# Self-attention on one core: GpSimd takes the rounding and the remainder of the first tile of probabilities

## The chip, the cores and the metric

One core of one Trainium2 chip. The metric is the device time of one execution of the kernel in microseconds (us).

## The reference

The input x is 8 sequences of 512 tokens with 256 channels, in float32. Two transformer layers follow each other. The first is a cross-attention layer (16 heads of 16, context of 64 tokens with 192 channels) and an MLP. The second starts with the self-attention that this change is about:

```python
def _attn(xq, xc, Wq, Wk, Wv, Wo, bo):      # HEADS 16, D_HEAD 64, xq = xc = layer norm of x
    q = (xq @ Wq).reshape(B, N, HEADS, D_HEAD)
    k = (xc @ Wk).reshape(B, S, HEADS, D_HEAD)
    v = (xc @ Wv).reshape(B, S, HEADS, D_HEAD)
    scores = jnp.einsum("bnhd,bshd->bhns", q, k) * D_HEAD ** -0.5
    attn = jax.nn.softmax(scores, axis=-1)
    out = jnp.einsum("bhns,bshd->bnhd", attn, v).reshape(B, N, HEADS * D_HEAD)
    return out @ Wo + bo
x = _attn(_ln(x, g1, b1), _ln(x, g1, b1), Wq1, Wk1, Wv1, Wo1, bo1) + x
```

A second cross-attention (on the context) and a gated MLP follow.

## The kernel before, in words

Every engine has a queue of its own, written out by hand, and waits for the others at counted events (`event`, `wait_ge`). To keep float32 accuracy with products in the faster float32r type, every operand is split in two: a rounded half, made by a copy (`act_copy` on ScalarE, `pool_copy` on GpSimd, line 159), and a remainder, the difference between the value and its rounded half (`dve_rest`, line 162, on VectorE; `pool_rest`, line 165, on GpSimd). A product is then three matmuls (`mm3`, lines 146 to 148): high by high, high by rest, rest by high.

The self-attention runs over 64 steps (`loop3`): 8 sequences by 8 pairs of heads. In step `s` three things overlap, each on another pair of heads: the pair `t = s` has its scores and exponentials computed, the next pair `u = s + 1` is projected (queries, keys, values) and its largest scores are found, and the pair before, `d = s - 1`, is multiplied with its values. Each step has four parts, `j = 0` to `3`, one per tile of 128 keys. A tile of probabilities is 128 keys by 1024 (two heads by 512 queries), and goes this way:

1. TensorE makes the scores in two parts (`scores`, lines 1348 and 1352); the second part waits for the negated maxima of the pair.
2. ScalarE takes the exponential (line 1500) into one of two buffers, `pst3[n % 2]`. It may start once the remainder of the tile two before has been made, since that read the same buffer.
3. The tile is rounded into `P3[0]`: by ScalarE for `j` = 1 and 2, by GpSimd for `j` = 0 and 3. The product with the values of the pair before must have read the old tile (`d3_mm`).
4. VectorE makes the remainder of all four tiles into `P3[1]` (`rests`, line 1582, by the helper of line 162). Its queue takes the remainder of tile 3 early in the next step.
5. TensorE multiplies both with the values, one step later (`values`).

VectorE's queue in a step is: remainders of the next queries (line 1569, two of 64x512, one input in PSUM), the reciprocals of the sums (line 1615), the remainder of the previous step's tile 3, remainders of the next keys (line 1573, two), remainder of the next values (two of 128x256), remainder of tile 0, in even steps an addition to x (line 1636), the largest scores of the next pair (line 1588, a reduction of 128x1024 from PSUM), and so on with the remainders of tiles 1 and 2 between the reductions; in odd steps the addition to x stands near the end. TensorE's `largest` (line 1386) makes the scores that these reductions read and waits for the remainders of the next queries and keys. After the fourth reduction TensorE transposes the maxima (line 152) and ScalarE negates them.

GpSimd's queue in a step is: two copies of the next keys (64x512 each, `k3_dup`), the rounding of tile 0, then at `j = 2` the product of the previous output with the reciprocals (line 1697, waits for a DMA), its rounding and its remainder (128x512), and the rounding of tile 3. Every eighth step (`p == 6`, an even step) also normalises the next sequence: an addition to x that GpSimd starts at the end of the step before (line 283), and a rounding and a remainder of 128x1024.

SP's queue issues the DMAs of the sums and reciprocals, which wait for events of VectorE and ScalarE.

Of the kernel before, what the change touches and what calls it, by code (L numbers as in the profile page):

```python
# [102 lines left out]
def f32(ap):  # L103
    return ap.bitcast(FP)
# [6 lines left out]
def build(nc, x, ctx_in, par, con, bias, wts, out):  # L111
    es = ExitStack()
    with es:  # L113
# [291 lines left out]
        with nc.sbuf_tensor("R3", [128, 24576], FR) as r, nc.sbuf_tensor("F3", [128, NALL - 24576], FP) as g:  # L405
# [4 lines left out]
            P3 = ra.pair(4, 2 * NT)  # L410
# [789 lines left out]
        p3_act, p3_pool, p3_lo = event("p_act", 2 * N3), event("p_pool", 2 * N3), event("p_lo", 4 * N3)  # L1200
# [53 lines left out]
        def pool_values(b, half):  # L1254
            pool.wait_ge(vw_hi, 2 * b - 4 + half)
            v = vw_b[b % 2][:, 4 * half:4 * half + 4]
            pool_rest(v[:, :, 1], f32(v)[:, :, 1], v[:, :, 0]).then_inc(vw_lo.sem, 1)

# [75 lines left out]
        def pe_attention1():  # L1334
# [54 lines left out]
            def values(d, j):  # L1389
                pe.wait_ge(p3_lo, 4 * d + j)  # L1390
                pe.wait_ge(v3_lo, 2 * (d // 2) + j // 2)
                if j == 0:
                    pe.wait_ge(d3_out, d - 1)
                    pe.wait_ge(gelu, NM - 1)
                vh, vl = v3_s[(d // 2) % 2]
                for h in range(2):
                    cs = slice(64 * h, 64 * h + 128)
                    m = mm3(bank(4 + h), (vh[:, j, d % 2, cs], vl[:, j, d % 2, cs]),
                            [v[:, j, NT * h:NT * h + NT] for v in P3], j == 0, j == 3)
                m.then_inc(d3_mm.sem, 1)  # L1400
# [77 lines left out]
        def act_attention1():  # L1478
# [17 lines left out]
            def exponent(t, j):  # L1496
                n = 4 * t + j
                act.wait_ge(c3_mm, n)
                act.wait_ge(p3_lo, n - 2)
# [62 lines left out]
        def dve_attention1():  # L1562
# [13 lines left out]
            def rests(n):  # L1576
                if 0 <= n < 4 * N3:
                    if n % 4 in (1, 2):
                        dve.wait_ge(p3_act, 2 * (n // 4) + n % 4 - 1)
                    else:  # L1580
                        dve.wait_ge(p3_pool, 2 * (n // 4) + n % 4 // 3)
                    dve_rest(P3[1][:, n % 4, :], pst3[n % 2], P3[0][:, n % 4, :]).then_inc(p3_lo.sem, 1)
# [72 lines left out]
        def pool_attention1():  # L1655
# [22 lines left out]
            for s in loop3:  # L1678
# [9 lines left out]
                for j in range(4):  # L1688
                    if ok(u, N3) and j == 0:
# [13 lines left out]
                    if ok(t, N3) and j in (0, 3):  # L1703
                        pool.wait_ge(e3, 4 * t + j)
                        pool.wait_ge(d3_mm, 4 * (t - 1) + j)
                        pool_copy(P3[0][:, j, :], pst3[j % 2]).then_inc(p3_pool.sem, 1)
# [57 lines left out]
        def sp_attention2():  # L1764
# [3 lines left out]
            for i in loop4:  # L1768
                b = i // 4
                if i == 2:  # L1770
                    sp.wait_ge(p3_lo, 4 * N3 - 1)
# [365 lines left out]
```

## Time and profile before

| | |
|---|---|
| median of 3 runs | 2293.42 us (2293.42 to 2293.97) |
| the profiled execution | 2292.69 us, span 2290.9 us |
| mean granted TensorE clock | 0.98 |
| TensorE busy | 2121.8 us (93%) |
| VectorE busy | 1608.8 us (70%) |
| ScalarE busy | 1482.3 us (65%) |
| GpSimd busy | 1070.5 us (47%) |

The span runs from the first to the last instruction of the profiled execution; the time also has what lies around it. The shares are means over stages with different limits: products, first layer, the self-attention loop, and the second half of the second layer. The times of rows count from the start of the span. A row of a stretch gives from and to, its length, the busy time (and instructions) of PE, PEld, DVE, ACT and POOL, the granted clock, the DMA share and GB/s. A row of the waits gives who waited for whom, the total in us, how often, and the longest. A row of a timeline gives the start, the duration, the engine, the line (often a helper's), the shapes, how many equal instructions were merged into it, and in brackets the engine's idle time before it and what ended that. PE is TensorE (PEld its weight loads), DVE is VectorE, ACT is ScalarE, POOL is GpSimd. A TensorE row lasts longer than the distance to the next one, because matmuls are pipelined.

### The profile page before, as it was taken

What the parts mean: (1) busy time and instruction counts of PE and PEld (TensorE: products, weight loads), DVE (VectorE), ACT (ScalarE), POOL (GpSimd) and SP (SyncE); (2) the same over time, 40 slices, a digit from 0 to 9 for tenths busy, and PEclk for the clock granted to TensorE, in tenths of its full rate; (3) what the DMA queues carried; (4) which work ended last, traced back from release to release, by engine and by line L of the source; (5) the groups of instructions that cost most, each with busy time, mean ns of one, the idle gap of its engine ahead of it and who ended that gap; (6) DMA issues with size and microseconds to landing.
All of it is one profiled execution on the core that took longest, in us unless ns stands there. A gap on an engine that the chain in (4) does not pass through costs nothing. (4 is left out here: it accounts for less than half of the span.)

```text
span 2290.9 us, 31305 instructions
## 1 busy us (share of the span) xinstructions
PE 2121.8 (93%) x11628; PEld 1771.6 (77%) x11628; DVE 1608.8 (70%) x2345; ACT 1482.3 (65%) x2154; POOL 1070.5 (47%) x819
## 2 busy tenths in 40 slices
PE   6868999988899999999999999999997799999998
PEld 4657888876687778777777777777776689888987
DVE  5576767753787787777877778778776766666553
ACT  5546888754777777777777777777774355554431
POOL 2154544441354454454544545545454665656432
PEclk8989999998999999999999999999999999999999
DMA  6810000010000100001001000010004411111000
GB/s 212 297 43 5 22 22 22 20 66 33 19 24 16 37 15 24 24 15 34 15 15 34 15 29 24 15 33 15 24 26 165 138 44 53 56 56 47 10 10 19
DMA packets 84280, 102.67 MB, mean 45 GB/s; under 512 B 29664, under 2 KB 61152, under 8 KB 83616
## 3 DMA queue, kind: packets, MB, share of 16 engines
q1 hardware_dynamic: 84128, 100.66, 13.3%
q8 instruction: 93, 1.52, 0.3%
q14 instruction: 59, 0.48, 0.1%
HBM read 65.50 MB, written 33.82 MB: 43 GB/s over the span
## 5 line engine op out<-in xcount | busy, mean ns | idle before, releaser
L146 PE MATMUL PS<-R 128*128 128x512 f32 (+1 forms) x2944 | 1026.4, 349 | 77.1 <-DVE R L162 46.1
L148 PE MATMUL PS<-R 128*128 128x512 f32 (+1 forms) x2944 | 996.5, 338 | 0.0
L147 PE MATMUL PS<-R 128*128 128x512 f32 (+1 forms) x2944 | 995.8, 338 | 0.0
L146 PEld LDWEIGHTS PS<-R 128*128 128x128 f32 x2944 | 565.8, 192 | 189.9 <-DVE R L162 55.3
L156 ACT ACTIVATE R<-PS 64x512 fp32r<-64x512 f32 (+4 forms) x860 | 460.1, 548 | 239.7 <-PE PS L1805 129.4
L148 PEld LDWEIGHTS PS<-R 128*128 128x128 f32 x2944 | 565.1, 192 | 60.4
L147 PEld LDWEIGHTS PS<-R 128*128 128x128 f32 x2944 | 566.9, 193 | 54.4
L162 DVE TENSOR_TENSOR R<-F,R 128x1024 fp32r<-128x1024 f32 (+2 forms) x416 | 465.2, 1123 | 44.2 <-ACT R L156 22.4
L159 POOL TENSOR_SCALAR R<-F 128x1024 fp32r<-128x1024 f32 (+1 forms) x295 | 266.2, 904 | 284.0 <-DVE F L1958 149.3
L1500 ACT ACTIVATE F<-PS 128x1024 f32<-128x1024 f32 x256 | 263.1, 1028 | 170.3 <-DVE R L162 115.1
L159 POOL TENSOR_SCALAR R<-R 64x512 fp32r<-64x512 f32 x128 | 142.8, 1129 | 391.4 <-ACT R L156 391.4
L1588 DVE TENSOR_REDUCE F<-PS 128x2 f32<-128x1024 f32 x256 | 301.4, 1214 | 14.1 <-PE PS L1386 14.1
L162 DVE TENSOR_TENSOR R<-PS,R 128x512 fp32r<-128x512 f32 (+3 forms) x348 | 181.0, 542 | 160.9 <-ACT R L156 160.3
L165 POOL TENSOR_TENSOR R<-F,R 128x512 fp32r<-128x512 f32 (+2 forms) x126 | 229.6, 1824 | 31.0 <-ACT R L156 22.4
L1569 DVE TENSOR_TENSOR R<-PS,R 64x512 fp32r<-64x512 f32 x128 | 88.0, 688 | 220.1 <-ACT R L156 220.1
L156 ACT ACTIVATE R<-F 128x1024 fp32r<-128x1024 f32 (+2 forms) x246 | 200.5, 829 | 61.2 <-PE PS L148 56.0
L156 ACT ACTIVATE F<-PS 64x512 f32<-64x512 f32 (+3 forms) x280 | 160.2, 593 | 50.4 <-PE PS L148 40.5
L1386 PE MATMUL PS<-R 128*128 128x512 f32 x512 | 164.0, 402 | 7.2 <-ACT F L156 4.9
L1352 PE MATMUL PS<-R 128*128 128x512 f32 x512 | 162.7, 399 | 7.8 <-ACT R L156 6.5
L1348 PE MATMUL PS<-R 128*128 128x512 f32 x512 | 165.9, 405 | 2.6 <-ACT F L1500 2.6
L1134 POOL TENSOR_TENSOR F<-F 128x1024 f32<-128x1024 f32 x32 | 67.9, 2123 | 165.4 <-DVE F L1048 165.4
L1697 POOL TENSOR_TENSOR F<-F 128x512 f32<-128x512 f32 x64 | 82.7, 1292 | 119.6 <-DMA F<-sd 119.6
(89 smaller groups left out, 1990.9 us busy)
## 6 DMA issues: line engine op xcount, KB each, us to landing
F<-sd SPq DMA_DIRECT2D x128, 128.0 KB, 2.8
xs<-F SPq DMA_DIRECT2D x16, 512.0 KB, 2.6
F<-xs SPq DMA_DIRECT2D x16, 512.0 KB, 3.6
gd<-F SPq DMA_DIRECT2D x8, 768.0 KB, 3.6
vd<-F SPq DMA_DIRECT2D x8, 768.0 KB, 5.9
R<-gd SPq DMA_DIRECT2D x6, 1024.0 KB, 5.5
R<-vd SPq DMA_DIRECT2D x6, 1024.0 KB, 5.7
F<-in_x SPq DMA_DIRECT2D x8, 512.0 KB, 5.7
```

Of the source, the lines that this page charges most:

```text
L146: nc.tensor.matmul(o, L[0], Rr[0], start=start, stop=False, skip_group_check=share)
L147: nc.tensor.matmul(o, L[0], Rr[1], start=False, stop=False, skip_group_check=share)
L148: return nc.tensor.matmul(o, L[1], Rr[0], start=False, stop=stop, skip_group_check=share)
L156: return nc.scalar.activation(o, i, ACT.Identity, **k)
L159: return nc.gpsimd.tensor_scalar(o, i, 1.0, 1.0, ALU.mult, ALU.mult)
L162: return nc.vector.tensor_tensor(o, i, f32(hi), ALU.subtract)
L165: return nc.gpsimd.tensor_tensor(o, i, f32(hi), ALU.subtract)
L1348: nc.tensor.matmul(bank(h), ka[i][h][:, kk], qa[i][h], start=True, stop=False)
L1352: m = nc.tensor.matmul(bank(h), kb[i][h][:, kk], qb[i][h], start=False, stop=True)
L1386: m = nc.tensor.matmul(bank(b0 + h), qa[i][h][:, 128 * q:128 * q + 128], ka[i][h], start=True, stop=True)
L1500: nc.scalar.activation(pst3[n % 2], bank(0, 2), ACT.Exp, scale=0.125).then_inc(e3.sem, 1)
L1588: nc.vector.tensor_reduce(M3[:, q, 0:128:64], bank(b0, 2).rearrange("p (a b) -> p a b", a=2), AX.X, ALU.max).then_inc(b3_max.sem, 1)
```

## The change

For tile 0 alone, GpSimd now makes both the rounded half and the remainder. It does so at the start of its part `j = 0`, ahead of the two copies of the next keys; before, it rounded the tile behind these copies, and VectorE made the remainder. VectorE makes the remainders of tiles 1 to 3. Since two engines now finish remainders, the event `p3_lo` is split in two, and `wait_rest3` picks the right one for a tile. The exponential that reuses a buffer, the value products and SP's first weight loads of the next stage wait by it.

```diff
--- before.py
+++ after.py
@@ -1197,7 +1197,8 @@
         nm3_mm, nm3_neg = event("nm_mm", N3), event("nm_neg", N3)
         c3_mm, e3 = event("c_mm", 4 * N3), event("exp", 4 * N3)
 
-        p3_act, p3_pool, p3_lo = event("p_act", 2 * N3), event("p_pool", 2 * N3), event("p_lo", 4 * N3)
+        p3_act, p3_pool = event("p_act", 2 * N3), event("p_pool", 2 * N3)
+        p3_lo_pool, p3_lo_dve = event("p_lo_pool", N3), event("p_lo_dve", 3 * N3)
         d3_mm, d3_sum, d3_out = event("d_mm", 4 * N3), event("d_sum", N3), event("d_out", N3)
         rec3, mul3, o3_hi, o3_lo = event("rec", N3), event("o_mul", N3), event("o_hi", N3), event("o_lo", N3)
         o3_mm, o3_add = event("o_mm", N3), event("x_add", N3)
@@ -1255,6 +1256,12 @@
             pool.wait_ge(vw_hi, 2 * b - 4 + half)
             v = vw_b[b % 2][:, 4 * half:4 * half + 4]
             pool_rest(v[:, :, 1], f32(v)[:, :, 1], v[:, :, 0]).then_inc(vw_lo.sem, 1)
+
+        def wait_rest3(queue, n):
+            if n % 4 == 0:
+                queue.wait_ge(p3_lo_pool, n // 4)
+            else:
+                queue.wait_ge(p3_lo_dve, 3 * (n // 4) + n % 4 - 1)
 
         def tail3(s, j):
 
@@ -1387,7 +1394,7 @@
                 m.then_inc(b3_mm.sem, 1)
 
             def values(d, j):
-                pe.wait_ge(p3_lo, 4 * d + j)
+                wait_rest3(pe, 4 * d + j)
                 pe.wait_ge(v3_lo, 2 * (d // 2) + j // 2)
                 if j == 0:
                     pe.wait_ge(d3_out, d - 1)
@@ -1496,7 +1503,7 @@
             def exponent(t, j):
                 n = 4 * t + j
                 act.wait_ge(c3_mm, n)
-                act.wait_ge(p3_lo, n - 2)
+                wait_rest3(act, n - 2)
                 nc.scalar.activation(pst3[n % 2], bank(0, 2), ACT.Exp, scale=0.125).then_inc(e3.sem, 1)
 
             def value(u):
@@ -1574,12 +1581,12 @@
                                                 ).then_inc(k3_lo.sem, 1)
 
             def rests(n):
-                if 0 <= n < 4 * N3:
-                    if n % 4 in (1, 2):
+                if 0 <= n < 4 * N3 and n % 4 > 0:
+                    if n % 4 < 3:
                         dve.wait_ge(p3_act, 2 * (n // 4) + n % 4 - 1)
                     else:
-                        dve.wait_ge(p3_pool, 2 * (n // 4) + n % 4 // 3)
-                    dve_rest(P3[1][:, n % 4, :], pst3[n % 2], P3[0][:, n % 4, :]).then_inc(p3_lo.sem, 1)
+                        dve.wait_ge(p3_pool, 2 * (n // 4) + 1)
+                    dve_rest(P3[1][:, n % 4, :], pst3[n % 2], P3[0][:, n % 4, :]).then_inc(p3_lo_dve.sem, 1)
 
             def largest(u, q, b0):
                 dve.wait_ge(b3_mm, 4 * u + q)
@@ -1686,6 +1693,12 @@
                     for b_ in (6, 7):
                         pool.wait_ge(x_out[x_at(0, b_)], store_no[0, b_])
                 for j in range(4):
+                    if ok(t, N3) and j == 0:
+                        pool.wait_ge(e3, 4 * t)
+                        pool.wait_ge(d3_mm, 4 * (t - 1))
+                        pool_copy(P3[0][:, 0, :], pst3[0]).then_inc(p3_pool.sem, 1)
+                        pool.wait_ge(p3_pool, 2 * t)
+                        pool_rest(P3[1][:, 0, :], pst3[0], P3[0][:, 0, :]).then_inc(p3_lo_pool.sem, 1)
                     if ok(u, N3) and j == 0:
                         for h in range(2):
                             pool.wait_ge(k3_hi, 2 * u + h)
@@ -1700,10 +1713,10 @@
                         pool_copy(o3_s[f % 2][0], OA).then_inc(o3_hi.sem, 1)
                         pool.wait_ge(o3_hi, f)
                         pool_rest(o3_s[f % 2][1], OA, o3_s[f % 2][0]).then_inc(o3_lo.sem, 1)
-                    if ok(t, N3) and j in (0, 3):
-                        pool.wait_ge(e3, 4 * t + j)
-                        pool.wait_ge(d3_mm, 4 * (t - 1) + j)
-                        pool_copy(P3[0][:, j, :], pst3[j % 2]).then_inc(p3_pool.sem, 1)
+                    if ok(t, N3) and j == 3:
+                        pool.wait_ge(e3, 4 * t + 3)
+                        pool.wait_ge(d3_mm, 4 * (t - 1) + 3)
+                        pool_copy(P3[0][:, 3, :], pst3[1]).then_inc(p3_pool.sem, 1)
                     for job in weights3_at(s, j):
                         pool_weight(job)
                     for _ in range(early4_pool.get(tail3(s, j), 0)):
@@ -1768,7 +1781,8 @@
             for i in loop4:
                 b = i // 4
                 if i == 2:
-                    sp.wait_ge(p3_lo, 4 * N3 - 1)
+                    wait_rest3(sp, 4 * N3 - 4)
+                    wait_rest3(sp, 4 * N3 - 1)
                     for k in range(4):
                         sp_weight(g5, k)
                     sp_load(3, 2, xs)
```

## Rows read from the trace of the kernel before

**Rows 1.** Busy time by stretch: an odd step, an even step, the whole loop.
```profile
1181.99:1199.82 17.83, 17.81 (x91) 14.45 (x90) 13.33 (x16) 13.79 (x20) 8.42 (x7) 1.00 0.06 16
1199.82:1218.36 18.54, 17.47 (x88) 14.04 (x87) 14.12 (x16) 13.70 (x21) 7.55 (x7) 1.00 0.12 44
573.00:1756.00 1183.00, 1130.17 (x5625) 910.97 (x5626) 908.74 (x1119) 884.56 (x1291) 567.74 (x475) 1.00 0.08 26
```
**Rows 2.** The waits of the loop (573 to 1756 us), the longest.
```profile
POOL R L159 <- ACT R L156: 370.1, 63, 12.5
```
**Rows 3.** TensorE in order of time: start us, us, what, xcount [idle <-releaser].
```profile
1187.76 0.70 PE L1386 MATMUL PS<-R 128*128 128x512 f32 x2
...
1194.06 0.39 PE L148 MATMUL PS<-R 128*128 128x512 f32 x1
1194.46 0.36 PE L146 MATMUL PS<-R 128*128 128x256 f32 x1
...
1207.70 0.63 PE L1352 MATMUL PS<-R 128*128 128x512 f32 x2
1208.34 0.70 PE L1386 MATMUL PS<-R 128*128 128x512 f32 x2
...
1213.20 0.39 PE L148 MATMUL PS<-R 128*128 128x512 f32 x1
1214.52 0.65 PE L152 MATMUL PS<-F 128*128 128x128 f32 x4 [0.93 <-DVE F L1588]
...
1217.16 0.73 PE L1352 MATMUL PS<-R 128*128 128x512 f32 x2
```
**Rows 4.** VectorE in order of time, the same two steps.
```profile
1185.00 1.17 DVE L162 TENSOR_TENSOR R<-F,R 128x1024 fp32r<-128x1024 f32 x1
1186.20 1.41 DVE L1573 TENSOR_TENSOR R<-PS,R 64x512 fp32r<-64x512 f32 x2
...
1189.68 2.35 DVE L1588 TENSOR_REDUCE F<-PS 128x2 f32<-128x1024 f32 x2
...
1202.83 1.17 DVE L162 TENSOR_TENSOR R<-F,R 128x1024 fp32r<-128x1024 f32 x1
...
1205.70 0.76 DVE L162 TENSOR_TENSOR R<-PS,R 128x256 fp32r<-128x256 f32 x2 [0.26 <-ACT R L156]
1206.38 1.21 DVE L162 TENSOR_TENSOR R<-F,R 128x1024 fp32r<-128x1024 f32 x1
1207.51 0.68 DVE L1636 TENSOR_TENSOR F<-PS,F 128x512 f32<-128x512 f32 x1
```
**Rows 5.** ScalarE in order of time, the even step.
```profile
1204.10 1.03 ACT L1500 ACTIVATE F<-PS 128x1024 f32<-128x1024 f32 x1 [0.78 <-DVE R L162]
...
1212.57 1.03 ACT L1500 ACTIVATE F<-PS 128x1024 f32<-128x1024 f32 x1 [0.99 <-DVE R L162]
1213.63 2.27 ACT L156 ACTIVATE F<-PS 1x512 f32<-1x512 f32 x4
```
**Rows 6.** GpSimd in order of time, the even step.
```profile
1207.74 1.29 POOL L1697 TENSOR_TENSOR F<-F 128x512 f32<-128x512 f32 x1 [1.66 <-DMA F<-sd]
1209.12 0.62 POOL L159 TENSOR_SCALAR R<-F 128x512 fp32r<-128x512 f32 x1
1209.82 1.29 POOL L165 TENSOR_TENSOR R<-F,R 128x512 fp32r<-128x512 f32 x1
1213.75 1.04 POOL L159 TENSOR_SCALAR R<-F 128x1024 fp32r<-128x1024 f32 x1 [2.64 <-ACT F L1500]
```
**Rows 7.** A norm step (1272.8 to 1293.1 us): GpSimd, then VectorE, by time.
```profile
1272.33 2.40 POOL L283 TENSOR_TENSOR F<-F 128x1024 f32<-128x1024 f32 x1 [3.71 <-DVE F L262]
...
1287.49 2.37 POOL L165 TENSOR_TENSOR R<-F,R 128x1024 fp32r<-128x1024 f32 x1
...
1272.80 0.68 DVE L1569 TENSOR_TENSOR R<-PS,R 64x512 fp32r<-64x512 f32 x1 [0.55 <-ACT R L156]
...
1288.16 2.79 DVE L162 TENSOR_TENSOR R<-F,R 128x1024 fp32r<-128x1024 f32 x1
```

## Prediction

> **What bounds the kernel now.** I read the stretches first, then the waits, then two neighbouring steps engine by engine. The stretch from 573 to 1756 us is the self-attention loop: 1183 of the span's 2290.9 us for 64 steps, 18.5 us each with its edges [rows 1]. TensorE is busy in 1130 of the 1183 us; no other engine passes 909. In one odd step (17.83 us from 1181.99) and the even one behind it (18.54 us from 1199.82) TensorE is busy for all but 0.02 and 1.07 us. So the loop is TensorE's instruction stream plus the few places where its next instruction is not yet released. VectorE's 909 us don't bound by themselves; what matters is which of its results TensorE waits for.
>
> The waits [rows 2] say where GpSimd has room: it idles 370 us, 5.9 us each time, ahead of its copies, for ScalarE. Most of that lies ahead of the keys' copies, where the change puts its new work.
>
> TensorE's queue [rows 3] has a few soft places in two steps. Odd: the first L1386 (the products that the maxima are taken from) starts at 1187.76, in rhythm. The output product starts at 1194.46, while the 0.23 us rhythm from 1194.06 would have it at 1194.29: with the broken rhythm behind it 0.24 us, for GpSimd's rounded output. Even: an L1386 starts at 1208.34, 0.18 us later than the pair at 1207.70 needs, because VectorE's addition to x (L1636) ends only at 1208.19 [rows 4]; and the transposes start at 1214.52, 1.09 us later than the rhythm from 1213.20, for VectorE's last maximum. The last of these is worth little: ScalarE begins four copies of 2.27 us together at 1213.63 [rows 5], as soon as the value products of 1213.20 are done, and two more follow that L1352 waits for, at 1217.16. These 3.96 us from value product to L1352 hold whatever VectorE does.
>
> **The change, part by part.** Tiles 1 to 3 stay as they are. The waits that change their semaphore cost nothing: what they wait for comes earlier than before. For tile 0:
>
> VectorE loses its remainder, 1.21 us at 1206.38 in the even step [rows 4], the same in the odd one. If nothing else moved, the x addition would come early enough to give back 0.18 us and 0.07 of broken rhythm, and ScalarE's chain leaves the transposes 0.05: 0.3 us an even step. The output wait of the odd step could give its 0.24. That is the whole prize: (0.3 + 0.24) x 32 = 17 us.
>
> GpSimd rounds tile 0 ahead of the keys' copies. Behind exponential 3, which ends at 1212.57 + 1.03 = 1213.60 [rows 5], its rounding starts at 1213.75 [rows 6], 0.15 later. So behind exponential 0 (1199.82 + 1.03 = 1200.85) it starts at 1201.00 and ends 1.04 later. The value product that must have read the old tile lies at the start of the step and is over. 0.08 us on (as from 1209.12 + 0.62 to 1209.82) the new remainder starts, at about 1202.13. It takes what the same instruction on the same shape takes in the layer norm, 2.37 us [rows 7], to 1204.50.
>
> **The collision.** VectorE wants its remainder of the previous tile 3 at 1202.83, in the odd step at 1185.00 [rows 4]: both 3.0 us after exponential 0 starts. GpSimd's will have started 0.70 us before. Rows of the norm step show this very pair [rows 7]: GpSimd's started at 1287.49 for 2.37 us, VectorE's at 1288.16, and VectorE's took 2.79 us instead of 1.17; it ended 1.09 us after GpSimd's. The first to start runs, the other stands. The Trainium skill, SBUF — State Buffer, "Who interferes with whom", has this as a rule, and it speaks against the change: a VectorE instruction with two SBUF inputs and a GpSimd one that reads SBUF want one port pair, and the first holds it for its whole length. By that rule VectorE would end a full instruction behind GpSimd, 0.1 us later than the row, and the sum would be some 3 us higher; the trace agrees but for that 0.1. VectorE's other operations around there have one input in PSUM; one of them (1272.80, 0.68 us) lies inside a GpSimd addition of 2.40 us [rows 7] and keeps its length. Only the remainder collides.
>
> It ends, then, at 1204.50 + 1.09 = 1205.59 instead of 1202.83 + 1.17 = 1204.00: **1.59 us late**. Behind it in VectorE's queue stand the keys' remainders (L1573), the values' rests, the x addition and the maxima; and ScalarE's exponential 1, which started at 1204.10 after 0.78 us of waiting for that same remainder [rows 5].
>
> Odd step. L1573 starts at 1186.20 + 1.59 and takes 1.41, to 1189.20. L1386 needs it and wanted 1187.76; with 0.07 for the release it starts at 1189.27: TensorE stands 1.51 us. Then VectorE has caught up, because tile 0's remainder is gone: the first maximum, at 1189.68 before, now waits for TensorE. The output product comes 1.5 us later, so its 0.24 vanish. Net +1.27.
>
> Even step. Exponential 1 starts at 1205.69; the values' copies and rests follow it as before, the rests at 1205.70 + 1.59 for 0.76, to 1208.05; the x addition then runs to about 1208.65 instead of 1208.19. L1386 starts at 1208.80 instead of 1208.34: +0.46. Behind that the maxima keep pace, and the fixed 3.96 us carry the 0.46 into the next step.
>
> The keys' copies (2.3 us together without a block, 1.1 more with VectorE first behind GpSimd's remainder) end near 1207.9. Their readers are the scores of the next step: nothing. The product with the reciprocals (L1697) waited for its DMA until 1207.74: 0.1 to 0.2 late, hidden by the same step's TensorE delay. SP's queue is not passed: the reciprocal that starts its DMAs stands ahead of the blocked remainder.
>
> Every eighth step is the norm step, even. There GpSimd starts with the addition at 1272.33 for 2.40 us [rows 7], which moves tile 0's rounding to about 1274.8 and the remainder to 1275.9. VectorE's wants 3.0 us after 1272.80, at 1275.8: a tie, VectorE first by 0.1. Then nothing is late and the 0.25 at the x addition is gained, some -0.2 us. If GpSimd wins, about +1.
>
> **Sum.** Eight steps: 4 x 1.27 + 3 x 0.46 - 0.2 = 6.3 us; times eight, 50 us. The profiled execution took 2292.69 us (span 2290.9 and 1.8 around it), 0.7 below the median of 2293.42; 2292.7 + 50 = **2343 us**, 2.2% more.
>
> **Rivals.** (A) No collision, because VectorE's remainder is first: the prize of 17 us, 2276 us. For it: 0.7 us of lead is not much beside what moves elsewhere. Against it: both engines count from the same exponential, and GpSimd would have to start 0.7 us later behind it than the 0.15 of [rows 5, 6]. 6%. (B) The collision is there, and TensorE's slack of 1.1 us in two steps takes it up: within 0.2% of 2293. For it the even step's 1.09; against it that this wait lies behind the delay, and that the odd step has no slack ahead of L1386. 3%. (C) Exponentials and maxima re-form around the stall and it counts by half: 2318 us. 15%. (D) Neither delay is caught up: with exponential 1 late, tile 1's remainder runs into GpSimd's output remainder (1.29 us at 1209.82 [rows 6]) in every step, and the tie in the norm step is lost. Then odd steps cost 1.5, even ones 1.0, the norm step 1: 4 x 1.5 + 3 x 1.0 + 1 = 10 us in eight steps, 80 in all, 2373 us. 12%. (E) The sum above: 64%.
>
> **How the numbers follow.** Within 0.2% (4.6 us) a measurement of this kernel can't be told from no change. Faster is A, 6%; no change is B, 3%; slower is the rest, 91%. The unknown inputs of E are the tie (-0.2 or +1 a norm step, 10 us) and the even step (0.3 to 0.9 for 0.46, 15 us). The range takes these and C in, and leaves out A, B and the far part of D: 2316 to 2362 us.
>
> **What the changed profile should show.** GpSimd's 128x1024 remainders in the loop: 64 more, near 2.4 us. VectorE's: 192 instead of 256, a third of them (those behind the reciprocal) near 2.6 us instead of 1.17. In the odd step L1386 directly behind L1573, with 1.5 us of TensorE idle ahead that names VectorE. Odd steps of 19.1 us, even ones of 19.0. If VectorE's remainders stay near 1.2 us, the collision was wrong and A holds. If they are long and the odd step still takes 17.8, it is B. If the even step has grown by 1 or more, D.

## The result, and the profile after

The changed kernel takes 2337.34 us in the median of four runs, the kernel before 2293.42 us. One of the four was in a slow state (2652.71 us, at a mean granted clock of 0.745 where the others have 0.98); the other three took 2334.98 to 2339.24 us. Those three, against the runs of the kernel before, give a ratio of 1.0192 with a 95% interval of 1.0172 to 1.0212: 1.9% slower. The profiled execution took 2339.24 us, with a span of 2337.4 us.

The stretches, in the columns of [rows 1]: an odd step, the even one behind it, the whole loop.

```profile
1205.66:1224.79 19.13, 17.86 (x92) 14.60 (x91) 14.59 (x15) 13.65 (x20) 9.83 (x8) 1.00 0.06 15
1224.79:1243.72 18.93, 17.74 (x88) 14.11 (x87) 14.53 (x15) 13.64 (x20) 9.83 (x8) 1.00 0.12 43
573.00:1802.00 1229.00, 1136.07 (x5626) 915.29 (x5625) 943.22 (x1056) 880.54 (x1291) 689.83 (x539) 1.00 0.08 25
```

The two steps took 17.83 and 18.54 us and now take 19.13 and 18.93. In the odd step nearly all of the growth is idle time of TensorE, 1.27 us where it was 0.02. In the even step the idle time went from 1.07 to 1.19 us, and the other 0.27 us show as busy time (17.74 for 17.47). The 256 exponentials give the loop as a whole (count, duration, first and last start), before and after:

```profile
L1500 ACT ACTIVATE F<-PS x256: 1007/1027/1035, 573.4 to 1741.8; 128x1024 f32<-128x1024 f32 x128
L1507 ACT ACTIVATE F<-PS x256: 1004/1027/1033, 575.1 to 1788.0; 128x1024 f32<-128x1024 f32 x128
```

From first to last start that is 1212.9 us, where it was 1741.8 - 573.4 = 1168.4: 44.5 us, nearly all of the 46.6 us by which the two profiled executions differ. From each exponential 0 to the next (steps are numbered from 0), the 31 odd steps have a median of 19.08 us (17.82 before) and give 37.7 us, the 24 even ones 18.94 (18.55) and 8.3 us, the eight norm steps 20.10 (20.33) and -1.9 us. Exponential 0 starts these two steps at 1205.66 and 1224.79. In order of time, VectorE (L1580 was L1573 in the kernel before, L1595 was L1588, L1643 was L1636):

```profile
1208.68 2.71 DVE L162 TENSOR_TENSOR R<-F,R 128x1024 fp32r<-128x1024 f32 x1
1211.41 1.41 DVE L1580 TENSOR_TENSOR R<-PS,R 64x512 fp32r<-64x512 f32 x2
...
1213.76 2.57 DVE L1595 TENSOR_REDUCE F<-PS 128x2 f32<-128x1024 f32 x2
1216.24 1.98 DVE L162 TENSOR_TENSOR R<-F,R 128x1024 fp32r<-128x1024 f32 x1
...
1227.80 2.71 DVE L162 TENSOR_TENSOR R<-F,R 128x1024 fp32r<-128x1024 f32 x1
...
1232.88 0.68 DVE L1643 TENSOR_TENSOR F<-PS,F 128x512 f32<-128x512 f32 x1
```

GpSimd:

```profile
1206.77 1.05 POOL L159 TENSOR_SCALAR R<-F 128x1024 fp32r<-128x1024 f32 x1 [4.65 <-ACT F L1507]
1207.91 2.39 POOL L165 TENSOR_TENSOR R<-F,R 128x1024 fp32r<-128x1024 f32 x1
...
1225.90 1.04 POOL L159 TENSOR_SCALAR R<-F 128x1024 fp32r<-128x1024 f32 x1 [5.09 <-ACT F L1507]
1227.03 2.40 POOL L165 TENSOR_TENSOR R<-F,R 128x1024 fp32r<-128x1024 f32 x1
1229.40 2.18 POOL L159 TENSOR_SCALAR R<-R 64x512 fp32r<-64x512 f32 x2
```

GpSimd's remainder starts at 1207.91, VectorE's wants to at 1208.68, and takes 2.71 us instead of 1.17 [rows 4]. It ends at 1211.39, 1.09 us after GpSimd's 1210.30. The even step is the same: 1227.03 against 1227.80. The keys' remainders (L1580) start 1.54 us later than they otherwise would. TensorE, where L1393 is the former L1386 [rows 3]:

```profile
1212.97 0.70 PE L1393 MATMUL PS<-R 128*128 128x512 f32 x2 [1.27 <-DVE R L1580]
...
1233.71 0.70 PE L1393 MATMUL PS<-R 128*128 128x512 f32 x2
...
1239.52 0.66 PE L152 MATMUL PS<-F 128*128 128x128 f32 x4 [0.56 <-DVE F L1595]
```

In the odd step L1393 stands until 1212.97, 7.31 us after exponential 0 where it was 5.77 (1187.76 - 1181.99), and the row names the keys' remainder. In the even step the second L1393 starts 8.92 us after exponential 0, 8.52 before (1208.34 - 1199.82). ScalarE's exponential 1 in the even step waits 2.32 us, 0.78 before [rows 5]:

```profile
1230.61 1.03 ACT L1507 ACTIVATE F<-PS 128x1024 f32<-128x1024 f32 x1 [2.32 <-DVE R L162]
```

The waits of the loop. GpSimd's long wait ahead of the keys' copies [rows 2] is gone, since its own work stands there and now waits for the exponential, and a wait is new that the loop before does not have at all:

```profile
POOL R L159 <- ACT F L1507: 260.1, 56, 10.6
...
PE PS L1393 <- DVE R L1580: 42.5, 45, 1.6
```

In the norm step, the pair started in the other order by 0.04 us, VectorE (first row) ahead of GpSimd:

```profile
1304.02 1.17 DVE L162 TENSOR_TENSOR R<-F,R 128x1024 fp32r<-128x1024 f32 x1
...
1304.06 3.41 POOL L165 TENSOR_TENSOR R<-F,R 128x1024 fp32r<-128x1024 f32 x1
```

There VectorE keeps its 1.17 us and GpSimd pays, 3.41 instead of 2.4 us.

Such meetings are not new. The two engines meet in nearly every step of the kernel before as well. In its even step VectorE's remainder of tile 1 starts while GpSimd makes the remainder of the output (1209.82 to 1211.11 [rows 6]):

```profile
1210.37 1.82 DVE L162 TENSOR_TENSOR R<-F,R 128x1024 fp32r<-128x1024 f32 x1
```

It takes 1.82 us instead of 1.21 and ends 1.08 us after GpSimd's. Of the 22 even steps from 4 to 60 that are not norm steps, VectorE is held at tile 1 in 21. That is part of why the transposes wait 0.9 to 1.3 us there for its last maximum; in the one step without it (60) they wait 0.32 us. In the odd step VectorE is first (1191.95 for 1.22 us), and GpSimd's remainder of the output, 0.22 us behind, takes 2.14 us instead of 1.29. In the changed kernel VectorE comes later, so in the odd step it is now VectorE that is held (1216.24, 1.98 us).

### The profile page after: what moved, and what is told of

The parts are those of the page before. It is cut to its first block and busy times, and to the rows that moved or that the text cites. A ratio compares the mean times of both kernels' runs of the same rounds, so it can differ in the third digit from the quotient of the medians.

```text
span 2337.4 us, 31306 instructions
## 1 busy us (share of the span) xinstructions
PE 2130.4 (91%) x11628; PEld 1778.1 (76%) x11628; DVE 1642.0 (70%) x2281; ACT 1477.8 (63%) x2154; POOL 1192.3 (51%) x883
## 5 line engine op out<-in xcount | busy, mean ns | idle before, releaser
L146 PEld LDWEIGHTS PS<-R 128*128 128x128 f32 x2944 | 566.0, 192 | 178.6 <-DVE R L162 54.6
L148 PEld LDWEIGHTS PS<-R 128*128 128x128 f32 x2944 | 565.6, 192 | 61.3
L147 PEld LDWEIGHTS PS<-R 128*128 128x128 f32 x2944 | 567.2, 193 | 55.0
L162 DVE TENSOR_TENSOR R<-F,R 128x1024 fp32r<-128x1024 f32 (+1 forms) x352 | 489.6, 1397 | 45.6 <-ACT R L156 26.0
L165 POOL TENSOR_TENSOR R<-F,R 128x1024 fp32r<-128x1024 f32 (+2 forms) x190 | 366.0, 1928 | 39.6 <-ACT R L156 25.7
L1595 DVE TENSOR_REDUCE F<-PS 128x2 f32<-128x1024 f32 x256 | 305.1, 1216 | 20.0 <-PE PS L1393 16.1
L1393 PE MATMUL PS<-R 128*128 128x512 f32 x512 | 165.9, 405 | 48.9 <-DVE R L1580 42.5
L1393 PEld LDWEIGHTS PS<-R 128*128 128x128 f32 x512 | 88.7, 188 | 91.0 <-issue 68.5
L159 POOL TENSOR_SCALAR R<-R 64x512 fp32r<-64x512 f32 x128 | 128.3, 1017 | 20.9 <-ACT R L156 20.9
```

The lines of the kernel that those rows point to most:

```text
L146: nc.tensor.matmul(o, L[0], Rr[0], start=start, stop=False, skip_group_check=share)
L147: nc.tensor.matmul(o, L[0], Rr[1], start=False, stop=False, skip_group_check=share)
L148: return nc.tensor.matmul(o, L[1], Rr[0], start=False, stop=stop, skip_group_check=share)
L159: return nc.gpsimd.tensor_scalar(o, i, 1.0, 1.0, ALU.mult, ALU.mult)
L162: return nc.vector.tensor_tensor(o, i, f32(hi), ALU.subtract)
L165: return nc.gpsimd.tensor_tensor(o, i, f32(hi), ALU.subtract)
```

## The experiments

The kernel before ran beside every set on the same chip; a ratio is to those runs, with its 95% interval. "Before" is the kernel before the change, "the change" the changed one.

**1. The remainder behind the keys' copies** (on the change). The same work on GpSimd, at another place of its queue.

```diff
-                        pool.wait_ge(p3_pool, 2 * t)
-                        pool_rest(P3[1][:, 0, :], pst3[0], P3[0][:, 0, :]).then_inc(p3_lo_pool.sem, 1)
                     if ok(u, N3) and j == 0:
                         for h in range(2):
...
+                    if ok(t, N3) and j == 0:
+                        pool.wait_ge(p3_pool, 2 * t)
+                        pool_rest(P3[1][:, 0, :], pst3[0], P3[0][:, 0, :]).then_inc(p3_lo_pool.sem, 1)
```

> The changed kernel with one thing moved: GpSimd rounds tile 0 ahead of the keys' copies as in the change, but makes its remainder behind them. Collision theory: GpSimd's remainder now runs about 5.3 to 7.7 us after exponential 0, where VectorE has only instructions with one input in PSUM, so VectorE's 192 remainders go back to about 1.2 us except where they meet the output's remainder, L1580 and L1393 are back in rhythm, and what is left is the 17 us of prize that the prediction worked out: 2276 us, between 2268 and 2288. Rival (the remainder on GpSimd costs by itself, through later releases of the exponential of tile 2 or through GpSimd's fuller queue ahead of L1710): 2310 us or more, as the work that GpSimd does is the same as in the change.

Measured: 2288.42 us, ratio 0.9979 (0.9969 to 0.9989). The whole loss is gone and a little gained, with all of tile 0 still on GpSimd; the rival falls at its price of 2310. But 5 us are not the 17 of the prize. In the odd step VectorE now reaches its remainder of tile 1 sooner, and meets GpSimd's output chain there (L1711 is the former L1697); the last row is TensorE's in another odd step:

```profile
1189.56 1.58 DVE L162 TENSOR_TENSOR R<-F,R 128x1024 fp32r<-128x1024 f32 x1
...
1188.76 1.29 POOL L1711 TENSOR_TENSOR F<-F 128x512 f32<-128x512 f32 x1 [0.62 <-DMA F<-sd]
1190.14 1.48 POOL L159 TENSOR_SCALAR R<-F 128x512 fp32r<-128x512 f32 x1
...
677.95 0.36 PE L146 MATMUL PS<-R 128*128 128x256 f32 x1 [0.53 <-POOL R L165]
```

VectorE's remainder (1189.56) waits for the end of the product (1190.05), and then GpSimd's rounding takes 1.48 us instead of 0.62. So the output's remainder, for which TensorE waits in the odd step, mostly ends about 12.3 us after exponential 0, as before: the odd step gains nothing (17.87 us in the median for 17.82). In eight odd steps it is worse. There GpSimd's queue also has a small operation for the next sequence's norm (L256), behind the new remainder; the output's remainder ends at 12.8, TensorE stands 0.53 us for it, as in the last row, and the step takes 18.3 us. That is some 4 us in all, and is the rival's mechanism at a small price: GpSimd's fuller queue. The even steps gained what the prediction said, 0.28 us (18.27 for 18.55 in the median), where VectorE was not held at tile 1.

**2. One wait against the meeting** (on the change).

```diff
                         pool.wait_ge(p3_pool, 2 * t)
+                        pool.wait_ge(p3_lo_dve, 3 * t - 1)
```

> The changed kernel with one wait added: GpSimd's remainder of tile 0 starts only when VectorE has made the remainder of the previous tile 3. Collision theory: VectorE's remainder takes 1.17 us and L1393 of the odd step has its rhythm back (no 1.4 us of idle), but GpSimd's remainder runs at 4.2 to 6.6 us after exponential 0, the keys' copies at 6.7 to 8.9, and the product with the reciprocals is about 0.9 us later than its DMA would let it; the odd step's output product waits up to that. So 2276 plus up to 28: 2300 us, between 2280 and 2312. Rival (GpSimd's work itself is what delays, not the meeting of the two): no lower than the changed kernel, 2337 us or more, as everything on GpSimd is later still.

Measured: 2290.59 us, ratio 0.9989 (0.9979 to 0.9999). GpSimd's remainder and the keys' copies are both later than in the change, and the loss is gone; the rival falls. The number lies nearer to before than my 2300, for a reason in GpSimd's rows:

```profile
1182.69 1.17 DVE L162 TENSOR_TENSOR R<-F,R 128x1024 fp32r<-128x1024 f32 x1
...
1184.01 2.41 POOL L165 TENSOR_TENSOR R<-F,R 128x1024 fp32r<-128x1024 f32 x1 [2.16 <-DVE R L162]
1186.38 1.21 POOL L159 TENSOR_SCALAR R<-R 64x512 fp32r<-64x512 f32 x2
```

VectorE's remainder takes 1.17 us, GpSimd's follows, and then both keys' copies together take 1.21 us, where they took 2.29 before. Alone they cost 0.6 us each. The 2.29 already held a meeting with the same remainder of VectorE, in which GpSimd's copy was the one that stood, although the profile has it start 0.05 us ahead (in the even step, 1202.78 against 1202.83).

**3. The rounding alone** (on before): `pool_copy` of tile 0 ahead of the keys' copies, its remainder on VectorE as before.

```diff
+                    if ok(t, N3) and j == 0:
+                        pool.wait_ge(e3, 4 * t)
+                        pool.wait_ge(d3_mm, 4 * (t - 1))
+                        pool_copy(P3[0][:, 0, :], pst3[0]).then_inc(p3_pool.sem, 1)
                     if ok(u, N3) and j == 0:
...
-                    if ok(t, N3) and j in (0, 3):
+                    if ok(t, N3) and j == 3:
```

> The kernel before with only the first half of the change: GpSimd rounds tile 0 ahead of the keys' copies, VectorE makes all four remainders as before. The rounding ends at about 2.2 us after exponential 0, before VectorE's remainder of tile 3 wants to start at 3.0. Collision theory: nothing collides and nothing on a path moves, 2293 us within 4. Rival (moving the rounding ahead is part of the cost, by the keys' copies or by the wait for the value product): slower by 5 to 20 us.

Measured: 2292.62 us, ratio 1.0001 (0.9989 to 1.0013). That half of the change costs nothing that can be told from noise.

**4. The same place, but only writing** (on before, with the edit of 3 and, behind the rounding, this).

```diff
+                        for k in range(3):
+                            pool.wait_ge(p3_try, 3 * t + k - 1)
+                            nc.gpsimd.memset(f32(P3[1])[:, 0, 0:(1024, 1024, 512)[k]], 0.0).then_inc(p3_try.sem, 1)
```

VectorE's `rests` waits for the third before it makes tile 0's remainder over it.

> The kernel before with the rounding of tile 0 ahead of the keys' copies and, behind it, three fills of constants (1024, 1024 and 512 columns, about 2.4 us together) into the tile that VectorE's remainder overwrites later; VectorE makes all four remainders. GpSimd is as busy in the same place as in the change, and the keys' copies as late, but it reads nothing there. If it is GpSimd's reading of SBUF that VectorE's remainder meets: VectorE's remainders stay at 1.17 us and the time at 2293 within 5. Rival 1 (any GpSimd instruction in that place blocks, writing too): VectorE's remainders behind the reciprocal grow to 2.2 us or more and the time goes above 2340, since VectorE still has all four tiles. Rival 2 (the late keys' copies cost): above 2300 with VectorE's remainders at 1.17.

Measured: 2291.47 us, ratio 0.9995 (0.9985 to 1.0006). VectorE, then GpSimd:

```profile
1183.97 1.17 DVE L162 TENSOR_TENSOR R<-F,R 128x1024 fp32r<-128x1024 f32 x1
...
1183.06 2.55 POOL L1698 MEMSET R<- 128x1024 f32 x3
1185.58 1.20 POOL L159 TENSOR_SCALAR R<-R 64x512 fp32r<-64x512 f32 x2
```

GpSimd is busy from 1183.06 to 1185.61, VectorE's remainder lies inside that time and takes 1.17 us. Writing alone does not block it, and keys' copies that start at 1185.58 cost nothing. The Trainium skill, SBUF — State Buffer, "Who interferes with whom", says that an instruction of VectorE with two inputs in SBUF does not contend with one of GpSimd that only writes. These rows agree. A fill is not a remainder without its reading, so that it is the reading that blocks rests on this pair of operations.

**5. The collision without the relief** (on before, with the edit of 3): GpSimd makes the remainder early, as in the change, and VectorE makes it again in its old place.

```diff
+                        pool.wait_ge(p3_pool, 2 * t)
+                        pool_rest(P3[1][:, 0, :], pst3[0], P3[0][:, 0, :]).then_inc(p3_try.sem, 1)
...
+                    if n % 4 == 0:
+                        dve.wait_ge(p3_try, n // 4)
```

> The kernel before, with the rounding of tile 0 ahead of the keys' copies and GpSimd's remainder of tile 0 behind it, as in the change; but VectorE makes all four remainders as before, that of tile 0 a second time in its old place. This is the collision without the relief. Collision theory: VectorE's remainder behind the reciprocal takes 2.7 us, and as tile 0's remainder is still queued behind it, the 1.59 us are not caught up in either step: 1.5 us in 32 odd and 24 even steps, 84 us, 2377 us, between 2360 and 2395. Rival (the cost comes from readers that now wait for GpSimd's remainder, not from the meeting): as these readers wait for VectorE again here, no more than 2300.

Measured: 2432.74 us, ratio 1.0609 (1.0593 to 1.0625). The rival falls, but 142 us are much more than my 84, and outside my bounds. The late queue runs into a second meeting. VectorE, then GpSimd, in an odd step:

```profile
1213.47 2.73 DVE L162 TENSOR_TENSOR R<-F,R 128x1024 fp32r<-128x1024 f32 x1
...
1218.57 2.25 DVE L162 TENSOR_TENSOR R<-F,R 128x1024 fp32r<-128x1024 f32 x1
...
1212.70 2.41 POOL L165 TENSOR_TENSOR R<-F,R 128x1024 fp32r<-128x1024 f32 x1
...
1218.44 1.29 POOL L1706 TENSOR_TENSOR F<-F 128x512 f32<-128x512 f32 x1 [1.19 <-DMA F<-sd]
```

The first is the known one (2.73 us). The second remainder (tile 0's, 1218.57) now lands on GpSimd's product with the reciprocals (1218.44 to 1219.73) and takes 2.25 us. A delay of 1.6 us became 2.6, and the odd steps take 20.3 us for 17.8. The even steps from 4 to 60 come in three lengths, where the kernel before has one near 18.55: 20.1 us (5 of 22), in which tile 0's remainder is not held, 21.1 (11) and 22.7 (6), in which it is. What parts the last two was not followed up.

**6. Half the remainder** (on before, with the edit of 3): GpSimd makes the first 512 columns early, VectorE the other 512 late. Every reader of the tile waits for both.

```diff
+                        pool_rest(P3[1][:, 0, 0:512], pst3[0][:, 0:512], P3[0][:, 0, 0:512]).then_inc(p3_half.sem, 1)
...
+                    c0 = 0 if n % 4 else 512
+                    dve_rest(P3[1][:, n % 4, c0:], pst3[n % 2][:, c0:], P3[0][:, n % 4, c0:]).then_inc(p3_lo.sem, 1)
```

> The kernel before, with the rounding of tile 0 ahead of the keys' copies and behind it GpSimd's remainder of only the first 512 columns of tile 0 (1.29 us instead of 2.4); VectorE makes the other 512 columns in its old place. If VectorE is held exactly as long as GpSimd's instruction still runs: its remainder ends at 2.30 + 1.29 + 1.09 = 4.68 us after exponential 0 instead of 4.18, 0.5 us late instead of 1.6 (a duration of about 1.7 us), the odd step grows by 0.3 to 0.5 and the even one by nothing: 2302 us, between 2295 and 2310. Rival (each meeting has a fixed toll, whatever its length): VectorE's remainder 2.4 us or more and 2315 to 2340 us.

Measured: 2294.21 us, ratio 1.0011 (1.0002 to 1.002). VectorE, then GpSimd:

```profile
1204.31 1.61 DVE L162 TENSOR_TENSOR R<-F,R 128x1024 fp32r<-128x1024 f32 x1
...
1203.54 1.29 POOL L165 TENSOR_TENSOR R<-F,R 128x512 fp32r<-128x512 f32 x1
1204.81 2.17 POOL L159 TENSOR_SCALAR R<-R 64x512 fp32r<-64x512 f32 x2
```

GpSimd's ends at 1204.83, VectorE's 1.09 us later; 1.61 us, near the 1.7 expected. So the toll is the rest of the other's instruction (0.52 us, for 0.44 of delay; in the change 1.62, for 1.54) and not a fixed one. The time lies just below my bounds: of a delay of 0.45 us, 0.15 are left in an odd step (17.97 us for 17.82) and nothing in an even one.

**7 and 8. ScalarE's order** (7 on experiment 1, 8 on before): in even steps the negated maxima before the output's copies.

```diff
                         act_copy(OB[0:1, :], bank(5)[0:1, :]).then_inc(d3_sum.sem, 1)
+                        if ok(u, N3) and s % 2 == 0:
+                            act.wait_ge(nm3_mm, u)
...
+                            for h in range(2):
+                                m = act_copy(qb[u % 2][h][64:65, :], bank(odd_bank(u))[64 * h:64 * h + 1, :], scale=-1.0)
+                            m.then_inc(nm3_neg.sem, 1)
                         act.wait_ge(o3_lo, d - 1)
...
-                    if ok(u, N3) and j == 3:
+                    if ok(u, N3) and j == 3 and not (ok(d, N3) and s % 2 == 0):
```

> e1_rest_behind_keys (remainder of tile 0 on GpSimd behind the keys' copies) with ScalarE reordered in the even steps: the two negated maxima come before the two copies of the output (OA) instead of after them. It tests the step of the prediction that says that ScalarE's fixed chain, not VectorE's last maximum, sets L1359 in even steps. If so, L1359 comes 1.0 us earlier, the value products behind it then wait about 0.6 us for the output copies, and an even step loses 0.4 us: 2277 us, between 2268 and 2285. Rival (the value products' wait takes back all of it, or the chain was not the bound): 2288 within 3.

> The kernel before with ScalarE's reordering alone. There the transposes wait 1.1 us for VectorE's last maximum, so that the negated maxima can come only 0.8 us earlier than before, and the value products 0.2 us earlier: 2287 us, between 2280 and 2293. If the reordering gains as much here as on top of the remainder's move (10 us or more), the two are independent and VectorE's maxima were not the next bound behind ScalarE.

Measured: 2298.56 us (1.0034, 1.0022 to 1.0046) and 2304.01 us (1.0059, 1.0045 to 1.0072). Both miss, to the slow side. ScalarE in an even step of 7 (1200.80 to 1219.89):

```profile
1214.64 1.19 ACT L156 ACTIVATE F<-PS 1x512 f32<-1x512 f32 x2
1216.23 1.19 ACT L156 ACTIVATE R<-PS 1x512 fp32r<-1x512 f32 x2 [0.41 <-PE PS L152]
1217.45 1.20 ACT L156 ACTIVATE F<-PS 64x512 f32<-64x512 f32 x2
1218.67 1.19 ACT L156 ACTIVATE R<-PS 64x512 fp32r<-64x512 f32 x2
1219.89 1.03 ACT L1507 ACTIVATE F<-PS 128x1024 f32<-128x1024 f32 x1
```

The negated maxima (1216.23) now wait 0.41 us for the transposes with two output copies and two of the next queries still behind them, and exponential 0 stands behind all of these. Before, the output's copies filled that wait. An order that helps one reader put idle time into the engine that was itself without a break. But 7 has two kinds of even steps. In 11 of the 22 from 4 to 60 GpSimd's remainder of the output starts first and VectorE's remainder of tile 1 is held (2.15 to 2.34 us); the transposes are late, as in these rows, and the step takes 19.0 to 19.2 us. In ten VectorE is first, ScalarE doesn't wait for the transposes, and TensorE stands 0.4 to 0.6 us for the output's copies instead; the step takes 18.4 to 18.5, still more than the 18.26 of experiment 1. In 8, as before, VectorE is held in all but one, and nearly all take 19.0 to 19.3.

**9 and 10. The output's copies on VectorE** (9 on experiment 1, 10 on before), in even steps.

```diff
-                        act.wait_ge(o3_lo, d - 1)
...
+                        if s % 2:
+                            act.wait_ge(o3_lo, d - 1)
...
+                    if ok(d, N3) and j == 3 and s % 2 == 0:
+                        dve.wait_ge(d3_mm, 4 * d + 3)
+                        dve.wait_ge(o3_lo, d - 1)
+                        nc.vector.tensor_copy(OA[0:64, :], bank(4)[0:64, :])
+                        nc.vector.tensor_copy(OA[64:128, :], bank(5)[64:128, :]).then_inc(d3_out.sem, 1)
```

> e1_rest_behind_keys, and in even steps the two copies of the output (OA, 64x512 each) go from ScalarE to VectorE, behind its remainder of tile 2, into the time that the change freed there. e1's profile shows ScalarE without a break from 1212.06 to the next exponential 0 (1216.78) and TensorE waiting 1.0 us for it ahead of L1359, while VectorE idles 3.5 us. e7 showed that changing ScalarE's order only moves the wait; this takes 1.2 us off it. If ScalarE's chain is what bounds the even step of e1: L1359 about 1.0 and exponential 0 about 0.8 us earlier, 24 to 32 times: 2264 us, between 2258 and 2275. Rival (another wait takes over at once, as in e7, or VectorE's copies delay what stands behind them): 2283 or more.

> The kernel before with the output's copies of even steps on VectorE, as in e9. Here VectorE still makes tile 0's remainder, and its last maximum holds the transposes until 1214.5, behind which the next projection and exponential 0 stand. So the relief of ScalarE can give only 0.1 to 0.3 us an even step: 2287 us, between 2281 and 2293. That this and e1 alone give little but e9 gives 25 us or more would show that the two chains of the even step, VectorE's and ScalarE's, are nearly as long as each other, and that the prize of the change is cut by the second. Rival (ScalarE's chain alone bounds): 2270 or less here.

Measured: 2286.97 us (0.9982, 0.9972 to 0.9992) and 2294.15 us (1.0007, 0.9998 to 1.0015). Both miss: experiment 9 gave little where I expected 24 us, 10 gave nothing. But the profile of 9 has two kinds of even steps, ten of 17.4 to 17.5 us and twelve of 18.4 to 18.6 among the 22 from 4 to 60. For each: VectorE's remainder of tile 1, GpSimd's remainder of the output, TensorE's transposes.

```profile
1203.66 2.27 DVE L162 TENSOR_TENSOR R<-F,R 128x1024 fp32r<-128x1024 f32 x1
...
1203.56 1.29 POOL L165 TENSOR_TENSOR R<-F,R 128x512 fp32r<-128x512 f32 x1
...
1208.25 0.66 PE L152 MATMUL PS<-F 128*128 128x128 f32 x4 [1.23 <-DVE F L1596]
...
1384.66 1.22 DVE L162 TENSOR_TENSOR R<-F,R 128x1024 fp32r<-128x1024 f32 x1
...
1384.84 2.19 POOL L165 TENSOR_TENSOR R<-F,R 128x512 fp32r<-128x512 f32 x1
...
1388.20 0.66 PE L152 MATMUL PS<-F 128*128 128x128 f32 x4 [0.18 <-DVE F L1596]
```

In the first GpSimd started 0.10 us ahead, VectorE's took 2.27 us, and the transposes stood 1.23 us. In the second VectorE started 0.18 us ahead, GpSimd paid (2.19), and the transposes waited 0.18 us. Eleven of the twelve long steps are like the first (GpSimd 0.03 to 0.3 us ahead, VectorE's remainder 2.1 to 2.3 us; in the twelfth GpSimd's product with the reciprocals, late, holds it), and all ten short ones like the second.

The profile of 10 says why it gained nothing. It is the kernel before in this respect: in 19 of the 22 steps VectorE's remainder of tile 1 is held (1.7 to 2.1 us), and they take 18.3 to 18.7 us. In the other three VectorE is first, and they take 17.85 to 17.92 us. One of those, VectorE, then GpSimd:

```profile
768.94 1.21 DVE L162 TENSOR_TENSOR R<-F,R 128x1024 fp32r<-128x1024 f32 x1
...
769.01 2.30 POOL L165 TENSOR_TENSOR R<-F,R 128x512 fp32r<-128x512 f32 x1
```

**11 and 12. The second meeting ordered too** (11 on experiment 9, 12 on experiment 1).

```diff
                         pool.wait_ge(o3_hi, f)
+                        if ok(t, N3) and s % 2 == 0:
+                            wait_rest3(pool, 4 * s + 1)
```

> e9_output_on_vector with one wait added: in even steps GpSimd's remainder of the output starts only when VectorE has made its remainder of tile 1. In e9's profile the two want to start within 0.1 us of each other in each even step, and whichever is first there makes a step of about 17.4 or of 18.4 us: where GpSimd is first, VectorE's remainder takes 2.27 us and its last maximum, and with it the transposes, come 1.05 us later; where VectorE is first nothing waits for GpSimd's. If the order of starting is the cause, the wait makes all even steps short: some half of 24 steps by 1.0 us and the spread gone, 10 to 15 us below e9: 2273 us, between 2264 and 2280. Rival (the two kinds of steps have another cause, or holding GpSimd delays its rounding of tile 3 or the output): as e9 or slower, 2284 or more.

> e1_rest_behind_keys with the same added wait and the output's copies left on ScalarE. There the last maximum stands behind or beside ScalarE's chain, which ends the even step at 18.28 us in either order: 2288 us, between 2282 and 2290. A gain as large as e11's over e9 would show that the race and not ScalarE's chain bounded e1's even steps too.

Measured: 2269.74 us (0.9904, 0.9888 to 0.992) and 2284.14 us (0.9966, 0.9953 to 0.9978), both as expected. In 11 all 22 even steps from 4 to 60 are of the short kind, 17.44 to 17.50 us (same three rows, the step from 1183.04 to 1200.48):

```profile
1193.18 1.22 DVE L162 TENSOR_TENSOR R<-F,R 128x1024 fp32r<-128x1024 f32 x1
...
1194.55 1.29 POOL L165 TENSOR_TENSOR R<-F,R 128x512 fp32r<-128x512 f32 x1 [1.57 <-DVE R L162]
...
1196.72 0.65 PE L152 MATMUL PS<-F 128*128 128x128 f32 x4 [0.18 <-DVE F L1596]
```

In 12 all are at 18.26 to 18.29, where experiment 1 had nine of 22 at 18.45 to 18.57: there ScalarE's chain ends the step in either order. Experiment 11 is the best version: 1.0% below before. It keeps what the change does (tile 0 off VectorE), but how much of the gain is due to that was not measured: the kernel before with the output's copies on VectorE and the same wait was not run. Experiment 10's three steps of 17.9 us against 17.45 here are the only hint: as an estimate, some 0.4 us of the 1.1 that an even step gained come from tile 0, and the rest from the other two edits.

## Why the prediction was right

Sign, size and mechanism held: 2343 us were forecast, 2337 measured. By its steps:

- **The start of GpSimd's remainder.** Forecast 2.31 us after exponential 0 starts, with 0.70 us of lead. Measured 1207.91 - 1205.66 = 2.25 and 0.77.
- **The collision.** Forecast an end 1.09 us behind GpSimd's and 1.59 us late; measured 1.09 and 1.54. Experiment 1 has the same instruction elsewhere without the loss, 2 takes only the meeting away, 4 keeps GpSimd busy there without reading, and 6 shortens it: the meeting is the cause. That it is GpSimd's reading rests on 4 alone.
- **The odd step.** Forecast 17.83 + 1.27 = 19.1, with L1386 1.51 us later; measured 19.13 and 1.54. **The even step.** Forecast 19.0; measured 18.93, with the x addition ending 8.77 us after exponential 0 for a forecast 8.83.
- **The norm step.** A tie was forecast, VectorE first by 0.1; it was first by 0.04, in all seven norm steps from 6 to 54. At that margin the sign was partly luck; by the forecast some 10 us hung on it, inside the range.
- **The sum.** 50 us forecast, 44.5 measured in the loop. By kinds, between the first and the last exponential 0: 31 odd steps should give 39.4 us and gave 37.7, 24 even ones 11.0 and 8.3, eight norm steps -1.6 and -1.9. The sum counts one odd step more than that stretch holds, 1.3 us.
- **Rival C** (half) and **D** (not caught up) are out by the step lengths. But D's mechanism took place: with VectorE late, its remainder of tile 1 ran into GpSimd's output remainder in the odd steps of the changed kernel (median 1.88 us for 1.22 before). That it cost TensorE nothing there is the part of D that was wrong. In even steps it had been so before, and a later VectorE lost less by it (median 1.48 for 1.86), which helped to take up the delay.

Some readings were wrong without moving the number. I costed the keys' copies at "2.3 us together without a block"; that was with one, and alone they take 1.2 (experiments 2 and 4). They ended 6.8 us after exponential 0 (1229.40 + 2.18 - 1224.79), where I had 8.1. The output product of the odd step waited not for GpSimd's rounded output but for its remainder, which ended at 1192.17 + 2.14 = 1194.31. "Only the remainder collides" overlooked what the trace before had already: the meetings of the output's remainder with tile 1's, and behind them part of "VectorE's last maximum". And the "whole prize" of 17 us was not to be had by avoiding the first meeting: experiment 1 brought 5 us, because an earlier VectorE meets GpSimd's output chain (experiments 1, 9), and because GpSimd's fuller queue made eight odd steps longer. That ScalarE's 3.96 us are fixed whatever VectorE does was right only as long as VectorE delivers in time: after relieving ScalarE (9) the even step was still long wherever VectorE's last maximum was held. Experiment 10 shows the same on the kernel before: its three even steps in which VectorE was first took 17.9 us, where the one such step of the kernel before (step 60) took 18.53 like its neighbours; the held ones gained about 0.1 us. It takes both, ScalarE relieved and VectorE not held.

## What to carry to other kernels

Before giving GpSimd a share of VectorE's elementwise work, look for the instructions of VectorE with two operands in SBUF that want to start while GpSimd reads: the one that starts second waits out the other and loses up to nearly the other's whole length. An instruction whose duration takes two values in one profile is the sign to look for. Free time on GpSimd is worth what the overlap leaves; the same instruction, 3 us later in the queue, cost nothing. Where two such starts lie within 0.3 us of each other, add a wait that lets the engine on the critical path go first, and look for the next meeting each time a queue is moved.

## What the runs showed of the hardware

- A meeting costs the second one the remaining length of the first less about 0.1 us: 0.44 of 0.52 us (experiment 6), 1.54 of 1.62 (the change). VectorE then ends 1.09 us after GpSimd, and alone it takes 1.17 to 1.21. The wait shows as duration of the one that is held, not as idle time.
- A copy of 64x512 from SBUF on GpSimd takes 0.6 us alone; the two of a step that took 2.29 us together in the profile of before were one free copy and one that VectorE's remainder had held (1.70 us).
- GpSimd's fills with constants, 2.5 us around a two-operand instruction of VectorE, did not lengthen it.
- Which of two starts is first decided between even steps of two lengths in one execution, and with it about 1 us per step. In experiment 9 VectorE's remainder was held with GpSimd 0.03 us ahead by the profile (2.34 us), and free with GpSimd 0.01 us ahead (1.21 us).
- The order by the profile is not exact. GpSimd's copy of the keys (64x512), 0.05 to 0.06 us ahead of VectorE's remainder by the profile in even steps, was itself held in the kernel before (1.70 us, VectorE 1.17).
